# Output groups by strips of the convolution, and input transposes of neighbouring pixels, in a fused convolution kernel

## What is computed

```python
x = x + _L0_conv_ref(_gn(x), W_v, W_a, b_a, W_o, b_o)   # group norm, outlook attention
x = x + _L1_conv_ref(_gn(x), w)                          # group norm, depthwise 3x3 convolution
```

## Time and profile before

| | us |
|---|---|
| median of 3 runs (lowest, highest) | 5270.85 (5268.15, 5273.6) |
| the profiled execution | 5268.83 |
| its span, first to last instruction | 5266.6 |
| PE busy, idle waits not counted | 4189.2 (80%) |
| DVE busy | 4192.7 (80%) |
| ACT busy | 2035.5 (39%) |
| POOL busy | 3362.1 (64%) |
| mean granted clock of PE | 0.834 |

### The profile page before, as it was taken

How to read it: one execution, slowest core, us unless ns; L and a number is a source line. 1 busy time by engine, 2 the same in 40 slices (tenths; PEclk the granted TensorE clock), 3 DMA queues, 4 the chain that set the end, 5 groups by cost and what they waited for, 6 DMA issues and landing times.

```text
span 5266.6 us, 58011 instructions
## 1 busy us (share of the span) xinstructions
PE 4189.2 (80%) x13632; PEld 2149.8 (41%) x13632; DVE 4192.7 (80%) x4747; ACT 2035.5 (39%) x2881; POOL 3362.1 (64%) x3628
## 2 busy tenths in 40 slices
PE   4877887888887788887788877888877888878884
PEld 2434444444443444443444443444434444434442
DVE  5688787788787888877887878888778878788876
ACT  4334443244443344433444433444433444324421
POOL 5766766666666666666666656666666676666661
PEclk7988888888888888888888888888888888888876
DMA  1111111101111101111011111011111111110110
GB/s 38 37 35 25 46 42 37 46 18 41 46 33 46 37 23 46 46 33 46 21 39 46 35 44 45 15 46 46 33 46 25 34 46 39 40 46 15 44 37 19
DMA packets 126229, 195.55 MB, mean 37 GB/s; under 512 B 14248, under 2 KB 115464, under 8 KB 122472
## 3 DMA queue, kind: packets, MB, share of 16 engines
q1 hardware_dynamic: 97384, 155.50, 12.3%
q10 hardware_dynamic: 28672, 38.55, 2.4%
HBM read 39.22 MB, written 38.54 MB: 15 GB/s over the span
## 4 chain that ended last, share of the span: by engine, by line
PE 47%; DVE 25%; issue 18%; ACT 5%; DVEq 1%; DMA 1%; POOL 1%; ACTq 0%; SPq 0%; POOLq 0%; PEldq 0%; PEld 0%
PE acc L764 25%; PE bc L744 10%; DVE strip L657 9%; DVE prod L607 6%; PE side L709 6%; DVE top L633 3%; PE side L703 3%; DVE top L637 3%; DVE X L621 2%; ACT X L446 2%; PE side L715 1%; PE side L721 1%; DMA out<-tok_out 1%; ACT strip L540 1%; DVEq L249 1%
## 5 line engine op out<-in xcount | busy, mean ns | idle before, releaser
L764 PE MATMUL acc<-prod,wo 96*96 96x392 f32 x5312 | 2537.6, 580 | 340.6 <-DVE X L621 338.5
L607 DVE TENSOR_TENSOR prod<-bc,VAL 96x784 f32<-96x784 f32 x2048 | 1965.0, 964 | 805.5 <-PE bc L744 723.8
L369 POOL TENSOR_TENSOR prod<-prod 96x392 f32<-96x392 f32 x1440 | 1457.5, 1016 | 1328.0 <-DVE prod L607 1323.5
L744 PE MATMUL bc<-stack,sel 96*96 96x392 f16 x4608 | 1312.9, 381 | 525.4 <-DVE prod L607 508.8
L764 PEld LDWEIGHTS acc<-prod,wo 96*96 96x96 f32 x5312 | 987.0, 190 | 889.4 <-DVE X L621 502.9
L744 PEld LDWEIGHTS bc<-stack,sel 96*96 96x96 f16 x4608 | 589.9, 140 | 1473.9 <-DVE prod L607 824.0
L657 DVE SCALAR_TENSOR_TENSOR strip<-XP,sg,strip 96x448 f32<-96x448 f32 x1568 | 1062.9, 678 | 157.8 <-ACT strip L540 139.4
L351 POOL TENSOR_TENSOR att<-att,top 108x420 f32<-108x420 f32 (+1 forms) x576 | 590.8, 1044 | 162.3 <-DVE top L633 162.3
L439 ACT ACTIVATE att<-side,ba 108x420 f32<-108x420 f32 (+1 forms) x576 | 339.8, 595 | 915.5 <-PE side L709 868.2
L357 POOL TENSOR_TENSOR att<-att,top 108x420 f32<-108x420 f32 (+1 forms) x576 | 591.0, 1045 | 42.1 <-ACT top L473 42.1
L709 PE MATMUL side<-pooled,wa 96*108 96x392 f32 (+1 forms) x1152 | 508.4, 554 | 33.3 <-ACT pooled L498 20.5
(11 more groups left out here) (56 smaller groups left out, 2232.3 us busy)
## 6 DMA issues: line engine op xcount, KB each, us to landing
stack<-part SPq DMA_DIRECT2D x192, 275.3 KB
stack<-part SPq DMA_DIRECT2D x192, 256.9 KB
tok_in<-in_x SPq DMA_DIRECT2D x32, 1176.0 KB, 8.5
out<-tok_out ACTq DMA_DIRECT2D x224, 168.0 KB, 4.7
stack<-part SPq DMA_DIRECT2D x192, 30.5 KB
stack<-part SPq DMA_DIRECT2D x192, 28.5 KB
X<-in_L_conv_W_a SPq DMA_DIRECT2D x1, 364.5 KB
ACC<-select SPq DMA_DIRECT2D x1, 144.0 KB
```

The lines of the kernel that those rows point to most:

```text
L369: nc.gpsimd.tensor_tensor(p[:, 0, :], p[:, 0, :], p[:, 1, :], ALU.add).then_inc(pre_added, 1)
L607: nc.vector.tensor_tensor(prod[:, g % PRODUCTS, :, :].rearrange("c a (i j) -> c a i j", j=WIN), b, v, ALU.mult).then_inc(prod_ready, 1)
L744: last = nc.tensor.matmul(bc[g % 2][0:CH, a, 0:UNIT], sel[:, which, :], stack[h][:, qi, ki * TAPS + kj, si:si + HALF, sj:sj + WIN], start= ...
L764: last = nc.tensor.matmul(acc[0:CH, 0:UNIT], wo[:, :], prod[:, g % PRODUCTS, a, :], start=first, stop=s == LAST[c] and (g in PRE or t == 2 ...
```

## The change

Three things change. The input is loaded and transposed so that group k takes the 448 neighbouring pixels from 448k on, 112 for each transpose: partition p of tok_in has pixels 112t+p for t = 0 to 27. X0 is written without gaps. The output group k is strip k: transpose t takes pixels 448k+4p+t, and the store of a group writes one whole stretch of HBM, 112 pieces of 1536 bytes without gaps. Each output group waits for its own strip's taps, and the groups stand at g19+6k, two steps after the strip's last tap. Nothing else of the table is moved.

```diff
-    OUT: (55, 56, 56, 57, 59, 59, 60),
+    OUT: (19, 25, 31, 37, 43, 49, 55),
...
-        x_v = x.rearrange("b h w c -> b (h w) c").rearrange("b (p t) c -> b p t c", t=TT)
-        out_v = out.rearrange("b h w c -> b (h w) c").rearrange("b (p t) c -> b p t c", t=TT)
-        X0t = X0[:, :].rearrange("c (p t) -> c t p", t=TT)
+        x_v = x.rearrange("b h w c -> b (h w) c").rearrange("b (t p) c -> b p t c", p=TP)
+        out_v = out.rearrange("b h w c -> b (h w) c").rearrange("b (k p t) c -> b k p t c", k=STRIPS, t=4)
+        X0t = X0[:, :].rearrange("c (t p) -> c t p", p=TP)
         ACCf = ACC[:, :, :].rearrange("c h w -> c (h w)")
-        ACCt = ACCf.rearrange("c (p t) -> c t p", t=TT)
+        ACCt = ACCf.rearrange("c (k p t) -> c k t p", k=STRIPS, t=4)
...
-                act.dma_start(out_v[i - 1, :, 4 * k:4 * k + 4, :], tok_out[:, k % 2, :, :]).then_inc(y_out[k % 2], 16)
+                act.dma_start(out_v[i - 1, k], tok_out[:, k % 2, :, :]).then_inc(y_out[k % 2], 16)
...
-                    if k == 0:
-
-                        until(pe, tapped, upto(TAP_N, i, TAP_N))
+                    until(pe, tapped, upto(TAP_N, i, (KK - 1) * (k + 1)))
                     for t in range(4):
-                        last = nc.tensor.transpose(bank[0:TP, t * CH:(t + 1) * CH], ACCt[:, 4 * k + t, :],
+                        last = nc.tensor.transpose(bank[0:TP, t * CH:(t + 1) * CH], ACCt[:, k, t, :],
                                                    idn[0:CH, 0:CH])
```

## The result

| | before | after |
|---|---|---|
| median of 4 runs each, us (lowest, highest) | 5269.76 (5268.15, 5273.6) | 5428.84 (5424.88, 5438.81) |
| ratio after / before, 95% interval | | 1.0304 (1.0286 to 1.0321) |
| profiled execution, its span | 5268.83, 5266.6 | 5428.43, 5426.3 |
| mean length of a body in the loop | 160.6 | 166.5 |
| mean granted clock of PE | 0.834 | 0.83 |

The granted clock of PE stands as the share of full speed that the profile gives.

The account below looks back on a forecast made before the run. Neither PE nor DVE was taken to bound the whole; they wait for each other in turn. Terms summed to +3.4 us a body, +102 over 30 bodies, -9 at the ends: 5363 us, own range 5320 to 5390, wide range 5245 to 5470.

Parts of the forecast that it names:

- rival 1: The low clock stays at g35 to g37: +5.4 us there, +6.8 a body, 5466 us; chance 0.19.
- g19: PE waits 0.65 us for ACT's logits read, plus 0.40 for the output group: +1.05 us a body.
- the signs that the prediction named: Among them: body about 163.8 us, idle time at g36 up to some 3 us, at product 20 up by 1.
- Input side: ACT's shorter input reads at g5 to g10 gain almost nothing, and the load stays hidden: -0.2 us a body.
- Output groups leaving: Six of seven groups leave g55 to g60; only broadcast 61 starts earlier: -0.15 us a body.
- The taps: At the moved output groups each strip's taps have always run by then: waiting for them costs 0.
- g37: ACT's exponential stands behind the new output group's read, delaying DVE's first sum: +1.75 us a body at the high clock.
- The clock behind it: Term for PE's clock behind the moved groups, discussed at g58 to g63: +0.95 us a body.
- Ends: One output group left behind the last tap, -8.1 us; first body -1; -9 us in all.
- Rival 2: Groups in PE's idle gaps shorten low-clock stretches: around 5262 us, chance 0.17, or a clear gain to 5166, chance 0.11.
- Rival 3: The load of tok_in comes 2 us late at g5: 5423 us; chance 0.05.
- Rival 4: ACT reaches the exponential at g37 in time, leaving g19 alone: +0.7 us a body, 5283 us; chance 0.06.

Follow-up runs that it names:

- after_warm15: The kernel after with two extra matmuls, read by nobody, ahead of PE's wait at g15: 5359.99 us, ratio 1.0173.
- in_only: The kernel before with the input side of the change alone, output as before: 5454.84 us, ratio 1.0361.
- out_only: The kernel before with the output side of the change alone, input as before: 5365.8 us, ratio 1.019.
- best_more: g20_g38 with extra matmuls, read by nobody, at many steps where PE idles: 5013.67 us, ratio 0.9523.
- g20_g38: The kernel after with output group 0 at g20 instead of g19 and group 3 at g38 instead of g37: 5357.55 us, ratio 1.017.
- in_warm: in_only with two extra matmuls, read by nobody, ahead of PE's wait at g15: 5261.8 us, ratio 0.9988.
- in_slow: in_only with each of ACT's seven input reads done twice: 5391.98 us, ratio 1.0224.

## Why the prediction was right or wrong

The direction was right, the size too small: 5363 was forecast and 5429 measured, within the range from 5245 to 5470 and above the case's own one, 5320 to 5390. That the wide range holds it is in part luck: its upper end was there for rival 1, which did not happen. The case's own range is not what its bounds give, either: with g19 from +0.40 to +1.4 and the clock's term from -1.2 to +1.7 it would be 5279 to 5396. Of the signs that the prediction named all came but the length of the body.

- **Input side, -0.2 us a body: this step failed.** The facts that it rests on hold: ACT's write takes 536 ns (below) in place of 1001, the load is hidden, PE's wait at g9 goes, and DVE is the later one there. Even the -0.2 is to be found, in the 0.23 us of idle time that product 13 no longer has. The conclusion "worth almost nothing" doesn't follow. A wait that is taken from a place with cover does not vanish; PE gives the time to the next wait, at g15, and that one has no cover. It cost 2.3 us a body in the whole change (after_warm15) and 6.4 alone (in_only). The prediction had read the clock for g35 to g37 and g58 to g63, and reasoned on the clock behind the output groups, but it passed over the low clock of g9, which its own have in them (0.88 for g6 to g12), and did not ask where it would go.
- **Output groups leaving, -0.15:** right. The idle time ahead of product 61 fell from 0.16 to 0.01. ACT's waits for stores are gone and gained nothing. At broadcast 60 PE now waits for product 58 in place of tok_out.
- **The taps, 0:** right, and for a reason that doesn't hold. Broadcast g needs product g-2, that is product 17 for the group at g19, and the strip's last tap stands behind that product in DVE's order, not ahead of it. In the loop no group waited for a tap on PE all the same; the 34.0 us of such waits in the whole trace are in the last body.
- **g19, +1.05:** measured +1.29. The wait, 0.62 for 0.65, was exact; the four transposes took more than the 0.40 that I allowed (0.50 from their start to broadcast 20's), and the rest, 0.17, is hops.
- **g37, +1.75:** measured +2.08, with the mechanism and the order of events as told. The 3.7 for PE's work at the high clock was the author's estimate; in the kernel after 3.8 us lie between the end of the addition and the group (2829.37 to 2833.17), 0.40 between the group's start and the next broadcast's, and 0.16 between the end of the read and the issue. Rival 1, the low clock at g35 to g37, did not come: there it was high in all 30 bodies. The low clock came at other places, where I had not looked. The choice of the high clock was called a close one, and no run shows why it came out so.
- **The clock behind it, +0.95:** not found. No run shows this term, nor the +0.7 that rival 1 has for it; both were the author's estimates, not worked out from rows. What the runs showed in its place: out_only's body is 3.4 us longer (163.8 to 160.4 in the middle of the loop), and 1.29 and 2.08 are already that. The four terms of the output side add up to 3.6, so their sum was right, but by luck: two of them were 0.6 too small together and this one 0.95 too large.
- **Ends, -9:** the last tap ended 12.2 us before the end of the span before, and 4.1 after. That is -8.1, as worked out: the transposes took 0.87 us where 1.0 was put, and from the store's issue to the end it was 2.5. All of what lies outside the 30 bodies is 13 us shorter. The rows of the kernel after:

```profile
5421.50 0.68 DVE L657 SCALAR_TENSOR_TENSOR ACC<-XP,sg,strip 96x448 f32<-96x448 f32 x1
5422.32 0.87 PE L719 MATMUL side<-idn,ACC 96*112 96x96 f32 x4 [5.73 <-DVE ACC L657]
5423.76 0.32 ACTq L464 DMA_DIRECT2D out<-tok_out  x1
```

- **Rival 2, the clock gives the cost back:** it did not happen in the change. Its premise, that several us a body are to be had from PE's clock, is true, and larger than I gave: best_more takes 344 us less than g20_g38, 11 us a body, with the mean clock at 0.977 in place of 0.821. The groups in the gaps did not hold the clock (0.83 over the span of the kernel after); work placed for it does. (Its threshold of 2.8 us a body leaves out the two terms of -0.35.)
- **Rival 3, a late load:** ruled out. It landed in 7.8 us, and had some 23 until its first reader. The price of 106 ns for a piece was far too high: from out_only to the kernel after the queue's share goes from 12.0% of 5363.6 us to 12.9% of 5426.3 for 96768 packets more, an estimate of some 9 ns each. With no stores beside it, the load takes 7.8 us in pieces of 384 bytes (after) as in pieces of 10752 (out_only); with stores beside it, 10.3 and 9.4 us (in_only, in_warm) against 8.5 (before). So a cost shows only there, and it is hidden. The stores gained nothing by the pieces lying side by side: before, the first and the last store of a body take 2.1 us too, and only those between, which run beside each other and the load, take 4.1 to 7.8 (medians by their place in the body).
- **Rival 4, ACT not late:** ruled out by the 107.7 us.

## What to carry to other kernels

A wait that is off the critical path can stand in for a dearer one on it: here ACT's faster reads took PE's wait at g9 away (36.7 us in all before, 6.7 in in_only), PE idled for 2.64 us at g15 in place of 1.58, and the clock was low behind that in 26 bodies of 30 in place of 1. Before you take a wait away, follow where that engine's idle time goes next, and whether it comes ahead of a stretch that others wait for. Look at the granted clock of every stretch where PE is the later one; where it is low behind idle time, harmless matmuls in that idle time can be worth more than a reordering (here 344 us from g20_g38 to best_more, which is 4.8% below the kernel before), as long as they need nothing that is late itself. And when an in-order engine gets a new read in a step, it belongs behind the instruction that someone else waits for: one step in a table was 2.1 us a body.

## What the runs showed of the hardware

The clock was the surprise. in_only and in_warm have the same work but for 128 more PE instructions in in_warm, and in_warm is 193 us faster, at a mean clock of 0.831 in place of 0.80. PE's idle time ahead of the low clock at g15 was 2.64 us in in_only (low in 26 of 30 bodies) and 1.58 us in in_slow (in 22 of 30), with the engine 80 and 79% busy over the span. With 1.19 us there, in in_warm, the clock was high in all 30.

ACT's write of an input group, from the kernel after, with shapes kept apart (count, busy us, mean ns, idle before):

```profile
L446 ACT ACTIVATE X<-side 96x448 f32<-96x448 f32 x224 | 119.2, 536 | 51.2 <-PE side L715 50.0 <-ACT X L529 0.2
```

Against the earlier trace rows it is 536 ns in place of 1001 for the same 448 elements: with a step of 112 bytes between the written elements ACT took nearly twice the time. PE shows no such thing for its weight loads of ACC, which had a step of 112 bytes before and has 16 now (197 and 199 ns in the mean, with about a sixth of them at the low clock in both kernels).
